# Zero rows ahead of each expert's rows, and a last tile that reaches back, in a cross-attention, self-attention and mixture-of-experts kernel

## What is computed

```python
x = x + tanh(g_xattn) * xattn(layernorm(x), ctx)
s = layernorm(x)
x1 = _ln(s + attention(s), ln1_g, ln1_b)
# the experts: every row goes to its two best of 8
gates = softmax(x1 @ gW + gb);  top2_scores, top2_idx = top_k(gates, 2)
h = relu(einsum('nd,edf->enf', x1, W1) + b1[:, None, :])
y = einsum('enf,efd->end', h, W2) + b2[:, None, :]
ff = einsum('ne,end->nd', w, y)          # w: the two scores, zero elsewhere
x = x + tanh(g_ffn) * _ln(x1 + ff, ln2_g, ln2_b)
```

## Time and profile before

| what | value |
|---|---|
| median of the runs without a profile | 1204.14 us (1202.54 to 1205.6) |
| span of the profiled execution | 1214.7 us |
| PE busy | 1126.1 us (93%) |
| DVE, ACT, POOL busy | 827.8, 688.4, 265.8 us |
| attention, to the last row's destination on DVE | 0 to 897.5 us |
| plan and hand-over, to the first transpose on PE | 897.5 to 915.5 us |
| experts, to the last write-back issued | 915.5 to 1157.4 us |
| join | 1157.4 to 1214.7 us |

### The profile page before, as it was taken

The page is one execution under the profiler, slowest core; times in us unless marked ns, Lnnn a source line. Parts: engine busy times, 40 slices in busy tenths (PEclk is TensorE's granted clock), DMA queues, the critical chain, the costliest instruction groups (busy, mean ns, idle before and its releaser), DMA issues.

```text
span 1214.7 us, 36448 instructions
## 1 busy us (share of the span) xinstructions
PE 1126.1 (93%) x12924; PEld 840.5 (69%) x12925; DVE 827.8 (68%) x2431; ACT 688.4 (57%) x1186; POOL 265.8 (22%) x371
## 2 busy tenths in 40 slices
PE   6999999999999999999999999999728999999964
PEld 4576766676766666676666677667517999999942
DVE  5565777776777777667777776777744666666667
ACT  4666767677666667777667776776513333333200
POOL 1011111122212111222212221222321222222233
PEclk9999999999999999999999999999968999999988
DMA  6012043222111111111111011101056222222165
GB/s 149 22 42 68 17 123 105 69 68 74 40 33 37 51 34 33 38 41 34 33 53 38 10 45 46 30 28 64 28 116 187 71 69 71 72 72 71 52 212 159
DMA packets 66597, 79.18 MB, mean 65 GB/s; under 512 B 14008, under 2 KB 52536, under 8 KB 66328
## 3 DMA queue, kind: packets, MB, share of 16 engines
q1 hardware_dynamic: 52680, 54.24, 16.2%
q0 software_dynamic: 6096, 15.66, 3.9%
q10 hardware_dynamic: 7680, 7.34, 1.9%
HBM read 51.32 MB, written 25.90 MB: 64 GB/s over the span
## 4 chain that ended last, share of the span: by engine, by line
PE 75%; issue 9%; DVE 8%; ACT 4%; POOL 1%; DMA 1%; DVEq 0%; another core or an unknown queue 0%; SPq 0%; POOLq 0%; ACTq 0%
PE quad L1299 11%; PE bank L1289 10%; PE bank L1485 9%; PE quad L1497 9%; PE quad L1311 8%; PE sums L1322 6%; PE bank L1436 4%; PE bank L1389 4%; ACT probs L777 4%; PE quad L1308 3%; PE bank L1282 3%; PE bank L1457 2%; PE bank L1322 2%; DVE row_max_C L1050 2%; DVE row_max_C L1047 2%
## 5 line engine op out<-in xcount | busy, mean ns | idle before, releaser
L777 ACT ACTIVATE probs<-quad 125x1792 f32<-125x1792 f32 (+1 forms) x128 | 213.0, 1664 | 116.9 <-PE quad L1311 116.7
L855 ACT ACTIVATE scored_half<-quad 112x750 bf16<-112x750 f32 (+1 forms) x160 | 131.4, 821 | 89.5 <-PE quad L1299 89.0
L1037 DVE TENSOR_REDUCE row_max_A<-quad 112x2 f32<-112x750 f32 x128 | 120.1, 938 | 70.0 <-PE quad L1299 66.5
L1485 PE MATMUL bank<-tile_inT,tile_w 128*128 128x128 f32 x1008 | 124.4, 277 | 0.3 <-ACT tile_w L887 0.3
L1039 DVE TENSOR_REDUCE row_max_A<-scored_half 112x2 f32<-112x750 bf16 x128 | 118.6, 927 | 3.2 <-ACT scored_half L855 1.0
L1485 PEld LDWEIGHTS bank<-tile_inT,tile_w 128*128 128x128 f32 x1008 | 119.0, 194 | 0.7 <-ACT tile_w L887 0.7
L1497 PE MATMUL quad<-output_w,hiddenT 128*128 x504 | 119.1, 380 | 0.0
L1299 PE MATMUL quad<-kT_A,qT_A 32*112 32x375 f32 x1024 | 115.2, 519 | 3.5 <-ACT probs L777 1.5
L1216 DVE TENSOR_SCALAR hiddenT<-bank,hidden_b 128x128 f32<-128x128 f32 x252 | 71.0, 344 | 63.0 <-PE bank L1485 62.6
L1289 PE MATMUL bank<-ctxT,wxk 128*128 128x375 f32 x256 | 99.1, 510 | 5.5 <-DMA bxk<-in_bxk_dram 5.5
L739 POOL DMA_INDIRECT kept_dram<-tile_out,take_back x63 | 60.4, 959 | 186.3 <-DVE tile_out L1239 179.7
(11 more groups left out here) (225 smaller groups left out, 1995.0 us busy)
## 6 DMA issues: line engine op xcount, KB each, us to landing
ctxT<-in_ctxT_dram SPq DMA_DIRECT2D x32, 375.0 KB, 3.5
tile_in<-sent_dram SPq DMA_DIRECT2D x63, 129.0 KB
join_in<-kept_dram SPq DMA_DIRECT2D x28, 256.0 KB, 3.4
hidden_w<-in_hidden_w_dram SPq DMA_DIRECT2D x8, 512.0 KB, 5.0
output_w<-in_output_w_dram SPq DMA_DIRECT2D x8, 512.0 KB, 5.7
x_in<-in_x_dram SPq DMA_DIRECT2D x32, 112.0 KB, 2.9
x_res<-in_x_dram SPq DMA_DIRECT2D x32, 112.0 KB, 3.2
kept_dram<-x_shift SPq DMA_DIRECT2D x32, 112.0 KB
```

The source lines that it names most:

```text
L777: act.activation(probs[0:rows, t.buffer("probs", step), :, :], quad[0:rows, :, 0:U * T], ACT.Exp, scale=SCALE).then_inc(taken[kind_of(step ...
L855: act.activation(scored_half[:, t.buffer("half", step), 0:RT // 2 * n].rearrange("t (r s) -> t r s", s=n), quad[0:T, RT // 2:RT, 0:n], ACT ...
L1037: dve.tensor_reduce(row_max["A"][:, i:P // 2:ROWS], quad[0:T, 0:RT // 2, 0:S], AX_X, ALU.max).then_inc(taken[kind], 1)
L1485: mm = pe.matmul(hidden_bank[k][:, f * P:(f + 1) * P], tile_w[:, k, c, f * P:(f + 1) * P], tile_inT[:, k, c, :], start=c == 0, stop=c == D ...
```

## The change

In words:

- Every expert's rows now begin 128 rows (P) into its region. The 128 rows ahead of them are written with zeros by eight DMAs of SP, with fixed addresses, when item 5 is loaded. The zeros behind the last row, the copy `next_i`, the eight register loads and POOL's wait `tails_zeroed` are gone.
- An expert's tiles are read from the front, but the last begins 128 rows before the expert's end, so it reads some rows a second time (or, for an expert with under 128 rows, some of the zero rows ahead). Tiles past the last needed one read that same last tile.
- For each tile DVE works out how many of its first rows were done already (`tile_twice`). From that come two tables of 128 by 63: `row_is_new` (one or zero) and `spill_to` (the spill row where the row is not new). They are made after `table`, by way of one matmul on PE that spreads the 63 numbers over all partitions. In the loop one instruction on DVE takes the place of three.
- The number behind a row is no longer raised by one.
- SP reads the first tile's row number before it waits for the rows sent, not after.

```diff
@@ sync: one more block in turn(), the zeroing in E.rank is gone
-                    elif step == "E.rank" and t.item("E") == LAST_KNOWN:
-
-                        sp.wait_ge(rows_zeroed, 5)
-                        sp.wait_ge(rows_known, 1)
-                        for e in range(E):
-                            row_no = sp.value_load(next_i[0:1, e:e + 1], min_val=e * REGION, max_val=e * REGION + (LAST_KNOWN + 1) * T)
-                            sp.dma_start(io["sent"][bass.ds(row_no, BEHIND), :].rearrange("(p r) (h d) -> p (r h) d", r=4, h=2),
...
+                if n == 5:
+
+                    sp.wait_ge(rows_zeroed, 5)
+                    for e in range(E):
+                        sp.dma_start(io["sent"][e * REGION:e * REGION + P, :].rearrange("p (h d) -> p h d", h=2),
+                                     zero_row[:, :].unsqueeze(1).to_broadcast([P, 2, SENT // 2])).then_inc(margins_zeroed, DMA)
...
-            attention_over(sp)
+            sp.wait_ge(margins_zeroed, E * DMA)
             sp.wait_ge(table_ready, 1)
...
                     first = sp.value_load(table[0:1, bass.ds(n + NT, 1)], min_val=0, max_val=E * REGION - P)
+                    if t.base == 0:
+                        attention_over(sp)
@@ gpsimd
-                        if t.item("E") > LAST_KNOWN:
-                            pool.wait_ge(tails_zeroed, E * DMA)
...
+            pool.iota(spill_rows[:, :], pattern=[[P, NT]], base=SPILL, channel_multiplier=1).then_inc(rows_zeroed, 1)
@@ vector
-                        if t.item("E") == LAST_KNOWN:
-                            dve.tensor_copy(next_i[:, :], next_row[:, :]).then_inc(rows_known, 1)
...
-            dve.tensor_tensor(tile_rest[:, :], tile_count[:, :], counts[:, 0:1], ALU.add).then_inc(plan_steps, 1)
+            dve.scalar_tensor_tensor(tile_rest[:, :], tile_count[:, :], float(-P), counts[:, 0:1], ALU.add, ALU.add).then_inc(plan_steps, 1)
             step(14)
+            dve.tensor_scalar(tile_want[:, :], tile_row[:, :], float(P), None, ALU.mult).then_inc(plan_steps, 1)
...
+            dve.tensor_tensor(tile_twice[:, :], tile_want[:, :], tile_row[:, :], ALU.subtract).then_inc(plan_steps, 1)
...
+            dve.tensor_scalar(tile_row[:, :], tile_row[:, :], float(P), None, ALU.add).then_inc(plan_steps, 1)
             dve.wait_ge(table_turned, 1)
             dve.tensor_copy(table[:, :], rows_bank[0][0:1, 0:2 * NT]).then_inc(table_ready, 1)
+
+            dve.tensor_scalar(twice_diag[:, :], ident[:, 0:NT], tile_twice[:, :], float(P), ALU.mult, ALU.min).then_inc(twice_known, 1)
+            dve.wait_ge(twice_spread, 1)
+            dve.tensor_scalar(row_is_new[:, :], rows_bank[1][:, 0:NT], tile_f[:, :], None, ALU.is_le).then_inc(spill_known, 1)
...
+            dve.scalar_tensor_tensor(spill_to[:, :], row_is_new[:, :], 1.0, spill_rows[:, :], ALU.is_lt, ALU.mult).then_inc(spill_known, 1)
...
-                    dve.tensor_scalar(is_spill[:, :], meta[:, 1:2], 0.0, spill_row[:, :], ALU.is_equal,
-                                      ALU.mult).then_inc(spill_steps, 1)
-                    dve.wait_ge(spill_steps, t.item("D", 3, 1))
-                    dve.tensor_scalar(spill_row[:, :], spill_row[:, :], float(P), None, ALU.add).then_inc(spill_steps, 1)
-                    dve.scalar_tensor_tensor(take_back[:, k, :], meta[:, 1:2], -1.0, is_spill[:, :], ALU.add,
-                                             ALU.add).then_inc(spill_steps, 1)
+
+                    dve.scalar_tensor_tensor(take_back[:, k, :], meta[:, 1:2], row_is_new[:, bass.ds(n, 1)], spill_to[:, bass.ds(n, 1)],
+                                             ALU.mult, ALU.add).then_inc(taken_back, 1)
@@ tensor
+            pe.wait_ge(twice_known, 1)
+            pe.matmul(rows_bank[1][:, 0:NT], ones[0:NT, :], twice_diag[0:NT, :], start=True, stop=True).then_inc(twice_spread, 1)
...
+                    if t.base == 1:
+                        pe.wait_ge(spill_known, 1)
```

More of the change, by code:

```diff
@@ L283, in build @@
         zero_row = sb("zero_row", [P, SENT // 2])
-        next_i = sb("next_i", [P, E], I32)
         hidden_w = sb("hidden_w", [P, DC, E * F])
@@ L295, in build @@
         back_i = sb("back_i", [T, TOP], I32)
-        spill_row = sb("spill_row", [P, 1])
+        spill_rows = sb("spill_rows", [P, NT], I32)
         banks = [ctx.enter_context(nc.psum_tensor(f"bank{i}", [P, BANK], F32)) for i in range(3)]
@@ L377, in build @@
         tile_row, tile_rest = sb("tile_row", [P, 1]), sb("tile_rest", [P, 1])
+        tile_want, tile_twice = sb("tile_want", [P, 1]), sb("tile_twice", [P, 1])
+        twice_diag = sb("twice_diag", [P, NT], BF16)
+        row_is_new, spill_to = sb("row_is_new", [P, NT]), sb("spill_to", [P, NT])
         table = sb("table", [1, 2 * NT], I32)
@@ L735, in expert_turn @@
                     k = t.slot("D")
-                    pool.wait_ge(spill_steps, t.item("D", 3, 3))
+                    pool.wait_ge(taken_back, t.item("D", 1, 1))
                     pool.wait_ge(tile_done, t.item("D", 1, 1))
```

33 lines of the change are left out of this document (15 added, 18 removed).

## The result

Four executions of the changed kernel have a median of 1193.09 us (1191.11 to 1194.08) and four of the kernel before 1204.15 us (1202.54 to 1205.6): ratio **0.9904**, 95% interval 0.989 to 0.9918. The forecast was 1192.8 us. The experiments ran on three chips of the same kind, one for each group (experiments 1 to 4; 5 to 7; 8 to 10); on which chip the first result ran is not recorded. In the groups the kernel before took 1214.42, 1216.27 and 1216.9 us, about 1% more. Times of different groups are therefore compared only as ratios to the kernel before, which ran in each group, and traces by distances from one event. The profiled execution of the changed kernel is one of its four: 1193.44 us, with a span of 1191.7; the time is the span and 1.7 us around it.

A forecast was written before the change was run, and what follows sets the result against it. PE alone bounds the expert loop, so only the gap before it and the loop's ends can give time. Hand-over -10.9, last tile -0.3, opening and copy -0.15 sum to -11.35 us: 1204.14 to 1192.8 us, range 1189.5 to 1198.3.

The forecast's parts named there:

- The sends: End of attention: without the zeroing's wait POOL starts 0.82 us after DVE's last destinations, and the last send lands at 902.2.
- The hand-over: Attention to experts: SP's first register load runs ahead of the sends' landing; first tile issued at 902.45, 10.9 us earlier.
- The new tables: Behind the plan's table: four instructions of 0.3 us each, known at 902.2, costing nothing under a cover of 3.5 us.
- The loop and the last tile: Expert loop: three DVE instructions becoming one gains nothing beside busy PE; after the last tile it saves 0.3 us.
- Clock: Start of the experts: PE begins at half clock as before, so no change, with 1.5 us allowed either way.
- The early part: Opening and attention: dropped small instructions save 0.15 us; eight early zeroing DMAs take 7.6 us, hidden in SP's idle time.
- third rival: Early zeroing after 73.4 us delays the attention if issues exceed 3.1 us each; 4.5 us each cancels the gain; chance 2%.
- The page: POOL's last sends beside the plan: the skill page says working DVE could delay them; a trace row decided, no term taken.
- Sends held by the plan: POOL's last sends: DVE's plan instructions keep POOL out, sends end up to 2.3 us later, 1195.1 us; chance 7%.
- The zeroing's wait shorter without the profiler: Gap before the experts: zero rows land earlier in unprofiled runs, gain shrinks by 5.4 us to 1198.2 us; chance 12%.
- The change's own wait: Before the first tile: late new tables or item 31's x1_shift store become the last wait; 1195.8 at 3 us; chance 3%.
- fast end of the range: Whole kernel: 1189.5 us, allowing 1.5 us for the clock, 0.6 for a faster POOL start and 1.5 for spread.

The follow-up runs named there:

- experiment 1: The kernel before run once more with no edit: 1215.01 us, ratio 1.0002, with a profiled span of 1213.4 us.
- experiment 2: Changed kernel with the old zeroing put back at item 29, into a tensor nobody reads, and POOL's sends waiting for it: 1212.98 us, 0.9988 of before.
- experiment 3: Changed kernel with the old zeroing at item 29 into a tensor nobody reads, without POOL's wait for it: 1207.36 us, 0.9943 of before.
- experiment 4: Changed kernel with its short zeroing issued at the old late place, item 29, and POOL's sends waiting for it: 1202.88 us, 0.9904 of before.
- experiment 5: Changed kernel as it is: 1204.88 us, 0.9903 of before; then with SP's wait for the attention ahead of its register load again: 1207.08 us, 0.9924.
- experiment 6: Changed kernel with two more small DVE instructions in each tile of the expert loop: 1205.61 us, 0.9906 of before.
- experiment 7: Changed kernel with 18 filler matmuls on PE in the gap before the experts, nine before and nine after the plan's PE work: 1203.73 us, 0.99 of before.
- experiment 8: Changed kernel with the 18 filler matmuls in the gap and 26 more behind the last tile, ahead of the join: 1203.76 us, 0.9893 of before.
- experiment 9: Changed kernel with each of the eight early zeroings in 768 pieces instead of 256, same bytes: 1210.55 us, 0.9945 of before.
- experiment 10: Changed kernel with the old zeroing at item 29, unwaited by the sends, and the last x1_shift store on ACT's queue: 1208.67 us, 0.9933 of before.

## Why the prediction was right

Distances are from the start of the last send_row, since the two traces don't share a level.

| step | predicted | measured |
|---|---|---|
| first send of item 31 behind send_row's end | +0.82 | +0.82 (884.42 to 885.24) |
| last send landed | 4.85 | 4.83 |
| table ready | 3.75 | 3.75 (888.00) |
| SP issues the first tile | 5.10 | 5.14 |
| new tables known | 4.85 | 4.77 (spill_to done 889.02) |
| first transpose | 7.30 | 7.46 |
| sum against before | -10.9 | -10.73 |

Each step of the path came as worked out, to 0.2 us, and experiment 2 shows that the zeroing is the cause. The mechanism is right, and not only the number. That the forecast is 0.3 us from the measured median is luck in part: the traced pair gives 9.9 us behind the last send_row and the second pair 11.3.

**The sends.** The choice of 0.82 rather than 0.25 us for POOL's start was right, wherever POOL was free when send_row was done (experiments 3 to 10 have 0.81 or 0.82 as well). The argument was the kind of release: behind a result of another engine, not behind a landing.

**The hand-over.** The load ran ahead of the landing; experiment 5 prices it alone at 0.95 us, where my steps from the landing to the issue (1.05 before, 0.25 after) gave 0.8. What I had not seen is that the tile's load is not a constant: it took between 2.01 and 2.19 us where no zeros were moved beside it, and 0.13 us went against me here.

**The new tables.** Four instructions of 0.23, 0.23, 0.28 and 0.22 us, against 0.3 each. PE wanted them at 892.74, 3.7 us later: the cover was there, as wide as worked out (3.5 to 3.6).

**The loop and the last tile.** Nothing in the loop, as experiment 6 shows from the other side. Behind the last tile there are now 0.19 us from take_back to tile_sum where the earlier trace rows had 0.42, a gain of 0.23 against my 0.3:

```profile
1131.20 0.27 DVE L1235 SCALAR_TENSOR_TENSOR take_back<-tile_in,row_is_new,spill_to 128x1 uint32<-128x1 f32 x1 [0.72 <-PE quad L1502]
1131.39 0.41 DVE L1237 TENSOR_TENSOR tile_sum<-quad,output_b 128x256 f32<-128x256 f32 x1
```

**Clock.** PE started at half clock again, as forecast (granted 0.50 from 884 to 898 us). How long that lasts varies from profile to profile: in the chains the second group of 16 matmuls took between 1.79 and 2.54 us, and the first between 3.48 and 3.79 in those without fillers. In the traced pair it cost 0.78 us up to the third tile's matmuls, about half of the 1.5 that I allowed either way.

**The early part.** Nothing was lost: PE was busy for 31.85 of the 32 us from 73 to 105 us, in both traces. But the term was mis-sized: 5.35 us for eight issues, 0.67 each, where I took 0.95 from the old zeroing's line. The issue of 256 pieces was shorter than that of 704. More important, the *bound* of the third rival was wrong, although the rival didn't come about. I let SP's time decide ("over 3.1 us an issue" before anything is late, 4.5 to cancel the gain) and said that even the old pace would cost nothing. Experiment 9 has a mean of 1.66 us an issue and lost 5 us. The DMA engines had pieces to move for some 7 us after SP was free (560 packets under 512 bytes from 88 to 90 us, 175 still from 92 to 94), and the loss came on a path that my working did not have: not by x_in, but by PE, ACT and DVE standing at some time between 92.8 and 96.3. That the eight issues of the change stay clear of this was not shown by my working. The margin on the slow side was thinner than my 2% took it to be.

**The page.** The rule of the Trainium skill (page "SBUF — State Buffer", section "SBUF: two separate sides") by which a working VectorE can hold up GpSimd's descriptors would have made the sends longer. Both sends of item 31 run beside the plan's DVE instructions, and take 0.94 us each, as beside an idle DVE, and the last lands after 2.59 us where it was 2.57. This does not refute the page, since the trace doesn't tell whether any of the plan's instructions is of the kinds it names. They are short (0.07 to 0.28 us); for long ones no run here says anything.

**The rivals.** *Sends held by the plan*: no, as said. *The zeroing's wait shorter without the profiler*: it fell with experiment 1. Its basis was the step "no row tells where that difference lies", on the 10.6 us between span and median. It was the level on which the trace was taken, to all that experiment 1 shows, and likely that of the chip. Taking the same 11.35 us off the median was harmless, because the gain hardly depends on the level: beside each other the two kernels differ by 11.1 us at one level (1204.15 to 1193.09) and by 11.4 at another (1216.27 to 1204.88). The 12% that this rival got were too many: the profile of a kernel on the other level was read as the profiler's doing. *The change's own wait*: no, since x1_shift is stored early once SP is free.

**A slip.** The fast end of the range should be 1192.8 - 1.5 - 0.6 - 1.5 = 1189.2 us by its own terms, and not 1189.5. Nothing hangs on it.

What had no term in my prediction is how the 10.7 us divide. Experiments 2, 3 and 5 have a gap of 17.47 us with the zeroing waited for, 12.26 unwaited, and 7.41 without it. So **5.2 us were the wait, and 4.9 us the load that the zeros put on the DMA engines and SP**, 3.4 of them with the store out of SP's way (experiment 10). The kernel before has 17.93 and 18.19 us, 0.5 to 0.7 more than experiment 2. In the first trace that is the register load: from the landing to SP's issue it takes 1.05 us there and 0.30 in experiment 2. A change that had only dropped the wait would have got half.

## What to carry to other kernels

A large transfer that an engine waits for can cost twice: by the wait, and by what it does to the transfers beside it. Before dropping a wait, ask what is last then: here a short transfer that was waited for late cost nothing, and a long one that nobody waited for still cost half. When transfers are moved to a quiet place, count their pieces against the DMA engines until they have landed, not only the issuing queue's time: in experiment 9 the queue was free at 86.09 us, and the load of x_in, issued nearly 5 us later, still landed 6 us late.

## What the runs showed of the hardware

- **A small piece cost a DMA engine nearly as much as one three times its size.** 1 MB of zeros in 2048 pieces (516 bytes each: 129 KB in 256) took SP 5.31 us and disturbed nothing; in 6144 pieces of 172 bytes it took SP 13.24 us, and the DMA engines still had some at 92. What they moved, in 40 slices of the 10 us from 74 to 84, first in the changed kernel (experiment 5), then in experiment 9, with the engines' busy share above it:

```profile
DMA  9989899999899999999999999874422000000000
GB/s 360 378 275 306 250 299 291 252 190 109 101 149 126 140 153 118 126 124 126 126 140 147 140 105 118 124 83 74 50 39 33 17 0 0 0 0 0 0 0 0
```

```profile
DMA  6898999999999999999999999999999999999999
GB/s 180 348 420 276 254 223 231 181 95 56 52 53 56 52 48 45 43 56 50 43 59 61 54 61 48 45 43 48 79 51 39 50 54 50 64 49 61 61 51 50
```

  Where only zeros are moved, some 126 GB/s and 52 GB/s: 244 pieces of 516 bytes a us, or 302 of 172. In the changed kernel the engines are free by 82 us, 4 us before SP's next issue; in experiment 9 they are not free when it comes. The Trainium skill, page "DMA: Bandwidth & Descriptors", section "Specifications", says that transfers want at least 512 bytes for the full rate. The trace agrees in direction, though the 516-byte pieces, just above it, move at 126 GB/s only, a third of the 360 of the first slices, in which the 3000-byte rows of ctxT move too. Nothing of a jump at 512 bytes is to be seen here.
- **Another queue didn't shield.** Beside the zeros on SP's queue, an indirect DMA of POOL's queue landed after 5.38 us instead of 2.59 (experiment 10).
- **PE at half clock is paid in the next stage.** In experiment 7 nine filler matmuls took 4.00 us and the nine behind them 2.12; the first 16 real ones then took 2.05 us instead of 3.78. The gap that remains thus costs 7.4 us and some 2 us more. When the clock rises is not the same from run to run: in experiment 8 the second nine took 4.02.
- **Levels.** The kernel before had 1204.15, 1214.42, 1216.27 and 1216.9 us, the last three on three different chips, each within about 0.2%, and the ratio of the changed kernel to it was 0.9904 at the first level and 0.9903 at the third. A span that doesn't fit its median can be of another level.
